# TensorE work laid out product by product behind each burst of scores, with the layer norm and the next stage's start moved

## The chip, the cores and the metric

The kernel runs on one core of one Trainium2 chip. The metric is device time in microseconds (us), smaller is better. Engines are called as the profile calls them: PE is TensorE (matmuls), PEld its weight loads, DVE is VectorE, ACT is ScalarE, POOL is GpSimd, SP is the engine whose queue issues the DMAs.

## What is computed

The input `x` is 4 batches of 1024 tokens of 512 channels, float32. Four layers follow one another, each with a residual; each has 16 heads of 32 channels and a causal mask:

```
x = x + attn_a(layernorm(x))   # squared scores in place of softmax, divided by their sum, then @ Wo
x = x + ffn(layernorm(x))      # softmax attention; keys and values of a token are those of ONE head,
                               # picked by the argmax of softmax(x @ W_gate.T), values times that gate
x = x + attn_b(layernorm(x))   # softmax attention, one key and one value head shared by all heads,
                               # biases, then an output product
x = x + ffn(layernorm(x))
```

In `attn_a`, queries and keys are normalised per head (`(q*gamma+beta)` less its mean, over its deviation); the kernel folds the mean into the weights and the key's deviation into a scale.

## The kernel before

**Two programs.** One layer of one batch is a *stage*. The first program holds the 4 stages of `attn_a` (kind "squared"), the second the 12 stages of the other three layers (kinds "gated", "mqa", "gated"; the profile's names end in `_squared` and `_soft`). A stage has 4 *phases*, one for each group of 4 heads (NG = 4): 16 phases in the first program, 48 in the second. Phase `ph` belongs to stage `ph // 4`.

**A phase.** It has 10 bursts of scores for keys (`KEY_BURSTS`, event "keys", line 1078, in the second program preceded by line 1075, which lays the row's maximum into PSUM). Each burst fills two pairs of PSUM banks; ACT takes a pair with one exponential (line 775) or with squares (line 781). In the second program 9 bursts of the *next* phase's scores by rows lie between them (`ROW_BURSTS`, event "rows", line 1093); DVE takes their maxima (lines 862 and 867). Three pairs of PSUM banks go round: `need_pairs` makes PE wait at the start of a burst until the first pair of the burst before has been taken. POOL masks the probabilities (line 665) and adds them up (lines 678 to 688).

**Other TensorE work.** Everything else goes through two work banks of PSUM, one *unit* after the other, in turn: `av` (probabilities times values, line 1131, in the parts A, B and C), `sm` (sums, line 1106), `mxt` (transposed maxima, line 1197), `rs` and `rw` (line 1204, 1211), `ln` (transposes of the normalised tile, line 1139), `q`, `q2`, `k2` (queries and keys, line 1039), `kvar` (key variance, line 1182, after `ksq`, squares by POOL, line 721), `v2` (line 1174), `gt`, `gtt`, `kall`, `vall`, `kt` (gate logits, all keys and all values of a token block, keys transposed: lines 1052, 1162, 1046, 1190), `ks`, `vs`, `vst` (shared keys and values), `out` (line 1227 or 1229). A unit opens when the unit before the last has been taken out of its bank by ACT or DVE (`free`). In the list of the first program there are 272 units, in that of the second 952. Events without a unit: `load`, `rload` (DMAs), `stats` (DVE statistics at lines 884 to 887, POOL normalises the tile in place at lines 654 and 656), `add`, `mxr`, `gate`, `gate_exp`, `gate_value`.

**The order.** `plan` writes one list of events; every engine walks it in order and does its own part of each event. A phase is 20 *halves*: half 2k opens with the burst of keys k, half 2k + 1 with the burst of rows k. `phase` puts at fixed halves what belongs to the phase itself (av, sm, mxt, add and so on). What is free to move, here called filler, stands in `work` as (events, first half, last half), and `spread` deals it out over the 80 halves of a stage: it works out a pace from the weights of `WEIGHT`, the bursts' own weight among them, and issues filler while the half has room. Units named in `HALVED` are cut in two (an event "more" carries the first half of the products). `norm_events` puts the statistics of tile t + 3 just ahead of the transposes of tile t, and the transposes close together. The next stage's loads and layer norm stand in `work` after this stage's filler and the last stage's outputs; its keys and values may not begin before half 2 * HALVES + 5, which is in the stage's third phase:

```
work.append(([("load", s + 1, t) for t in range(TILES)] + norm_events(s + 1), 0, NG * HALVES))
work.append((first + rest, 2 * HALVES + 5, NG * HALVES))
```

`two_banks` sees to it that no more than two units are open: a third that starts ends the oldest one, with all its products, at once; so does any start after another unit has ended inside an open one.

Of the kernel before, what the change touches and what calls it, by code (L numbers as in the profile page):

```python
# [11 lines left out]
P = 128  # L12
# [66 lines left out]
HALVED = ("av", "q", "q2", "k2", "v2", "ks", "kall", "vall")  # L79
# [24 lines left out]
def features(ph):  # L104
    return [(u, ph, c) for c in range(NC) for u in ("q2", "k2", "ksq")] + [("kvar", ph, c) for c in range(NC)]


def keys_and_values(kind, s):

    if kind == "squared":  # L110
        first = [("v2", s, pair, n) for pair in range(2) for n in range(NT // 2)] + features(4 * s)
        return first, features(4 * s + 1)
# [7 lines left out]
    first = [("ks", s, 0), ("ks", s, 1)] + queries[0] + [("vs", s, 0), ("vs", s, 1), ("vst", s, 0), ("vst", s, 1)]  # L120
    return first, queries[1]


def halved(event, kinds):
    return event[0] in HALVED or event[0] == "out" and kinds[event[1]] != "gated"


def in_halves(events, kinds):
    return [e for event in events for e in ([("more", event)] if halved(event, kinds) else []) + [event]]


def weight(event, kinds):
    if event[0] == "more":
        return weight(event[1], kinds)
    share = 0.5 if halved(event, kinds) else 1.0
    if event[0] == "out":
        return share * (0.9 if kinds[event[1]] == "gated" else 3.5)
    return share * WEIGHT.get(event[0], 0.0)
# [11 lines left out]
def phase(kinds, ph):  # L150

    s = ph // NG
    at = [[] for _ in range(HALVES)]
    more = ph + 1 < NG * len(kinds) and kinds[(ph + 1) // NG] != "squared"
    for k in range(NKB):
        at[2 * k].append(("keys", ph, k))
        if more and k < NRB:
            at[2 * k + 1].append(("rows", ph + 1, k))
    if kinds[s] != "squared":
# [1132 lines left out]
```

How the kernel before makes its waits and increments, by code:

```python
        @block.gpsimd  # L355
# [1 line left out]
            pool.memset(k["ident"][:], 0.0).then_inc(sg.built, 1)  # L357
            pool.memset(k["ident16"][:], 0.0).then_inc(sg.built, 1)
            pool.memset(k["mask"][:], 0.0).then_inc(sg.built, 1)
            pool.memset(k["head_mean"][:], 1.0 / D).then_inc(sg.built, 1)
            pool.memset(k["ones"][:], 1.0)
            pool.memset(k["ones16"][:], 1.0)
            pool.memset(k["minus_half"][:], -0.5)
            pool.memset(k["eps2"][:], EPS * EPS)
            pool.iota(k["rank"][:], pattern=[[0, NT], [-1, HEADS]], base=HEADS, channel_multiplier=0,
                      allow_small_or_imprecise_dtypes=True)
            pool.wait_ge(sg.built, 4)
            for name in ("ident", "ident16"):
                pool.affine_select(out=k[name][:], in_=k[name][:], compare_op=ALU.not_equal, fill=1.0, base=0,
                                   pattern=[[-1, P]], channel_multiplier=1).then_inc(sg.built, 1)
# [2 lines left out]
            pool.affine_select(out=k["head_mean"][:], in_=k["head_mean"][:], compare_op=ALU.is_ge, fill=0.0, base=0,  # L373
                               pattern=[[-D, HG], [0, D]], channel_multiplier=1).then_inc(sg.built, 1)
            pool.wait_ge(sg.built, 7)
            pool.affine_select(out=k["head_mean"][:], in_=k["head_mean"][:], compare_op=ALU.is_ge, fill=0.0,
# [49 lines left out]
        @block.tensor  # L426
        def _(pe):
            pe.wait_ge(sg.loaded, everything)
            pe.wait_ge(sg.vector_step, 1)
            for u in range(2 * KC):
```

## Time and profile before

| | |
|---|---|
| median of 3 runs | 4739.77 us (4738.4 to 4744.24) |
| the profiled execution's own time | 4741.89 us |
| its span, first to last instruction | 4740.1 us |
| busy share of the span: PE, DVE, ACT, POOL | 81%, 40%, 34%, 63% |
| mean granted TensorE clock | 0.918 of full |

Busy time is the union of an engine's instructions. For a wait the profile names the instruction that ended it. A granted clock of 0.918 is a mean over two levels, full and half; a stretch with 0.90 has spent a fifth of itself at half.

### The profile page before, as it was taken

How to read it: one execution, taken by the hardware profiler on the slowest of the kernel's cores; microseconds unless marked ns; L12 is line 12 of the kernel's file. 1: busy time of each engine (PE TensorE's matmuls, PEld its weight loads, DVE VectorE, ACT ScalarE, POOL GpSimd, SP SyncE). 2: the span in 40 equal slices, each digit the busy share in tenths (PEclk: the TensorE clock that was granted, in tenths of full speed). 3: DMA queues.
4: the chain of work that ended last, by engine and by line, in shares of the span. 5: the costliest groups of instructions: out<-in, count | busy, mean ns of one | idle time of the engine just before them, and what ended most of it. 6: DMA issues, size and time to landing. Idle time of an engine off the chain costs nothing. (4 is left out here: it accounts for less than half of the span.)

```text
span 4740.1 us, 66857 instructions
## 1 busy us (share of the span) xinstructions
PE 3849.7 (81%) x26018; PEld 1585.2 (33%) x26018; DVE 1899.4 (40%) x4874; ACT 1630.1 (34%) x2433; POOL 2991.2 (63%) x2215
## 2 busy tenths in 40 slices
PE   6788888985978688688786888888798886977975
PEld 4343434322333233233232333333333332323332
DVE  1212212222544444444444445444544444544452
ACT  1543444551223223323333333333233233232333
POOL 2967777983254646547676676776557466465587
PEclk9899998987989889899898999999899997988998
DMA  1001010003000100100101010010001001010010
GB/s 62 18 1 37 18 36 19 19 19 103 18 1 1 54 1 8 48 1 21 34 17 38 1 34 21 23 32 25 30 1 54 1 19 36 1 53 2 1 37 27
DMA packets 63382, 115.05 MB, mean 24 GB/s; under 512 B 8672, under 2 KB 9184, under 8 KB 63072
## 3 DMA queue, kind: packets, MB, share of 16 engines
q1 hardware_dynamic: 63072, 110.77, 7.2%
q8 instruction: 212, 3.47, 0.3%
q14 instruction: 98, 0.80, 0.1%
HBM read 77.19 MB, written 33.55 MB: 23 GB/s over the span
## 5 line engine op out<-in xcount | busy, mean ns | idle before, releaser
L775 ACT ACTIVATE probs_soft<-banks 128x1024 f32<-128x1024 f32 (+1 forms) x960 | 848.6, 936 | 1426.0 <-PE banks L1078 1411.1
L688 POOL TENSOR_TENSOR added_soft<-added_soft,probs_soft 128x2048 f32<-128x2048 f32 (+3 forms) x384 | 1163.9, 3031 | 67.0 <-ACT probs_soft L775 47.9
L867 DVE CUSTOM_DVE_ANT_0 banks<-banks,mask 128x128 f32<-128x128 f32 (+3 forms) x1536 | 700.7, 525 | 739.1 <-PE banks L1093 739.1
L862 DVE TENSOR_REDUCE maxima_soft<-banks 128x2 f32<-128x1024 f32 x384 | 452.4, 1221 | 527.1 <-PE banks L1093 527.1
L1093 PE MATMUL banks<-k_soft,q_soft 32*128 32x512 f32 (+3 forms) x4608 | 531.4, 555 | 140.4 <-ACT probs_soft L775 140.3
L781 ACT ACTIVATE probs_squared<-banks,key_scale_squared 128x512 f32<-128x512 f32 (+3 forms) x768 | 379.2, 590 | 382.5 <-PE banks L1078 371.6
L665 POOL TENSOR_SCALAR_AFFINE_SELECT probs_soft<-probs_soft 128x512 f32<-128x512 f32 x384 | 239.7, 637 | 427.7 <-ACT probs_soft L775 427.6
L1078 PE MATMUL banks<-q_soft,k_soft 32*128 32x512 f32 (+3 forms) x4608 | 505.7, 521 | 0.0
L1131 PE MATMUL banks<-probs_soft,v_soft 128*32 128x512 f32 (+3 forms) x4608 | 454.2, 514 | 46.0 <-POOL probs_soft L665 31.7
L688 POOL TENSOR_TENSOR added_squared<-added_squared,probs_squared 128x2048 f32<-128x2048 f32 (+3 forms) x128 | 390.2, 3048 | 7.3 <-ACT probs_squared L781 1.9
L1075 PE MATMUL banks<-shift_soft,ones 32*128 32x512 bf16 (+3 forms) x2304 | 205.4, 344 | 227.2 <-DVE maxima_soft L867 136.4
L1093 PEld LDWEIGHTS banks<-k_soft,q_soft 32*128 32x128 f32 x4608 | 198.0, 199 | 378.6 <-issue 372.3
L681 POOL TENSOR_TENSOR added_soft<-probs_soft 128x2048 f32<-128x2048 f32 x48 | 216.8, 4518 | 123.0 <-ACT probs_soft L775 123.0
L1039 PE MATMUL banks<-xnT_soft,g_wq 128*128 128x512 f32 x512 | 254.9, 629 | 33.4 <-DVE scaled_out_soft L990 30.1
L1046 PE MATMUL banks<-g_wv,xnT_soft 128*128 128x512 f32 x512 | 247.9, 615 | 7.1 <-ACT k_soft L758 2.9
L1139 PE MATMUL banks<-ident,tiles_soft 128*128 128x128 f32 x384 | 81.2, 360 | 202.3 <-POOL tiles_soft L656 202.3
L1131 PEld LDWEIGHTS banks<-probs_soft,v_soft 128*32 128x32 f32 x4608 | 125.1, 112 | 353.7 <-issue 260.2
L1075 PEld LDWEIGHTS banks<-shift_soft,ones 32*128 32x128 bf16 x2304 | 64.9, 92 | 524.4 <-issue 505.0
L697 POOL CAST shift_cols_soft<-minus_max_soft 128x16 bf16<-128x16 f32 x96 | 24.4, 255 | 333.4 <-DVE minus_max_soft L875 333.4
L1078 PEld LDWEIGHTS banks<-q_soft,k_soft 32*128 32x128 f32 x4608 | 223.1, 195 | 25.6 <-issue 21.0
L1046 PE MATMUL banks<-g_wk,xnT_soft 128*128 128x512 f32 x512 | 223.8, 595 | 9.6 <-DVE picking_soft L846 9.6
L867 DVE DVE_READ_ACCUMULATOR2_ANT maxima_soft<- 128x1 f32 x1536 | 215.5, 140 | 0.0
(153 smaller groups left out, 4801.0 us busy)
## 6 DMA issues: line engine op xcount, KB each, us to landing
tiles_soft<-out SPq DMA_DIRECT2D x96, 256.0 KB, 2.9
rest_soft<-out SPq DMA_DIRECT2D x96, 256.0 KB, 3.0
out<-rest_soft SPq DMA_DIRECT2D x96, 256.0 KB, 2.1
tiles_squared<-in_x SPq DMA_DIRECT2D x32, 256.0 KB, 2.9
rest_squared<-in_x SPq DMA_DIRECT2D x32, 256.0 KB, 3.2
out<-rest_squared SPq DMA_DIRECT2D x32, 256.0 KB, 2.0
raw_wq<-in_squared_wq SPq DMA_DIRECT2D x1, 1024.0 KB, 5.6
raw_wk<-in_squared_wk SPq DMA_DIRECT2D x1, 1024.0 KB, 7.9
```

What stands on the lines that cost most here:

```text
L665: ins = pool.affine_select(out=cells, in_=cells, compare_op=ALU.is_ge, fill=0.0, base=0, pattern=[[0, HG], [1, P]], channel_multiplier=-1)
L688: ins = pool.tensor_tensor(sums, sums, slot(ph, n)[:, :, col:col + width], ALU.add)
L775: ins = act.activation(slot(ph, n)[:, 2 * a:2 * a + 2, 0:width], score_pair(e, a)[:, :, 0:width], ACT.Exp, scale=SCALE)
L781: ins = act.activation(slot(ph, n)[:, i, col:col + cols], score_pair(e, a)[:, x, col:col + cols], ACT.Square, scale=m["key_scale"][:, ph % ...
L862: ins = dve.reduce_max(m["maxima"][:, ph % 2, 2 * a:2 * a + 2, t, p], score_pair(e, a)[:, :, col:col + width], AX_X)
L867: ins = dve.tensor_tensor_reduce(scores, scores, k["mask"][:, CHUNK - width:CHUNK], 1.0, MASKED, ALU.add, ALU.max, m["maxima"][:, ph % 2, ...
L1039: ins = pe.matmul(out, wt[:, kc, cols], m["xnT"][:, kc, CHUNK * c:CHUNK * c + CHUNK], start=(kc == 0), stop=(kc == KC - 1))
L1046: ins = pe.matmul(out, m["xnT"][:, kc, P * t:P * t + P], wt[:, kc, cols], start=(kc == 0), stop=(kc == KC - 1))
L1075: pe.matmul(psum[:, score_bank(e, i), col:col + width], k["ones16"][D * i:D * i + D, :], m["shift"][D * i:D * i + D, ph % 2, c, q0:q0 + wi ...
L1078: ins = pe.matmul(psum[:, score_bank(e, i), col:col + width], k_of(ph)[D * i:D * i + D, P * kb:P * kb + P], m["q"][D * i:D * i + D, ph % N ...
L1093: ins = pe.matmul(psum[:, score_bank(e, i), col:col + P * blocks], m["q"][D * i:D * i + D, ph % NG, P * t:P * t + P], k_of(ph)[D * i:D * i ...
L1131: ins = pe.matmul(out[D * i:D * i + D, q0:q0 + width], left, slot(ph, n)[:, i, col:col + width], start=(x == 0), stop=(x == len(products) ...
```

## The change

The filler is cut into single products in place of halves (`PIECES`; `share` issues one product for each "more" and the rest at the end). `spread` no longer gives each half the same share: the share is now in proportion to a room per half, taken from `KEYS_TAKEN` and `ROWS_TAKEN` by the size of the burst, and the bursts' own weight is no longer counted. The fixed halves of `av` are kept, as two "more" in the first half and the rest in the second. The first half at which an event may stand comes from a new function `since`, per event: next-stage queries of group 0 from the second phase, those of group 1 from the third, everything that writes nothing in use from the start; the next stage is no longer held back to half 2 * HALVES + 5. The loads and the first four statistics of the next stage get places of their own at the stage's start; the transposes of tiles 0 to 3 alternate with the last stage's outputs 4 to 7, those of tiles 4 to 7 with parts of the next stage's first units. In the squared kind, `k2` and `ksq` now go before `q2`. In the gated kind, units of queries stand between the gate's steps, and `vall` comes last. ACT's guard at the first `ln` of a stage names `q2` in place of `k2`, as that is now the last reader.

```
-HALVED = ("av", "q", "q2", "k2", "v2", "ks", "kall", "vall")
+PIECES = {"av": 4, "q": KC, "q2": KC, "k2": KC, "v2": 2, "ks": KC, "kall": KC, "vall": KC}
+KEYS_TAKEN = {512: 1.25, 256: 0.85}
+ROWS_TAKEN = {P * n: (masked, plain) for n, masked, plain in ((1, 0.95, 0.4), (2, 1.2, 0.65), (3, 1.45, 0.95), (4, 1.75, 1.25))}

-def norm_events(s):
-    events = [("stats", s, t) for t in range(3)]
+def norm_events(s, between):
+    head = [("load", s, t) for t in range(TILES)], [("stats", s, t) for t in range(TILES)]
+    steps = []
     for t in range(NT):
-        if t + 3 < NT:
-            events.append(("stats", s, t + 3))
-        events.append(("ln", s, t))
-        if t + TILES < NT:
-            events.append(("load", s, t + TILES))
-    return events
+        steps.append([("ln", s, t)] + [("load", s, t + TILES)] * (t + TILES < NT))
+        if t >= 2 and t + 2 < NT:
+            steps[-1].append(("stats", s, t + 2))
+    between = [between[n::NT] for n in range(NT)] if len(between) > NT else [between[n:n + 1] for n in range(NT)]
+    return head, [steps[t] + between[t] for t in range(NT)]

 def features(ph):
-    return [(u, ph, c) for c in range(NC) for u in ("q2", "k2", "ksq")] + [("kvar", ph, c) for c in range(NC)]
+    return [(u, ph, c) for us in (("k2", "ksq"), ("q2",)) for c in range(NC) for u in us] + [("kvar", ph, c) for c in range(NC)]
...
-        first = [("gt", s, 0), ("gt", s, 1), ("gtt", s, 0), ("gtt", s, 1), ("gate", s), ("gate_exp", s), ("gate_value", s)]
+        first = [("gt", s, 1), ("gtt", s, 0), queries[0][0], ("gtt", s, 1), ("gate", s), ("gate_exp", s), queries[0][1], ("gate_value", s)]
         first += [("kall", s, t) for t in range(NT)]
         first.insert(len(first) - 2, ("krep", s, 0))
-        first += [("krep", s, 1), ("kt", s, 0)] + queries[0] + [("kt", s, 1)]
-        return first, [("vall", s, t) for t in range(NT)] + queries[1]
+        first += [("krep", s, 1), queries[1][0], ("kt", s, 0), queries[1][1], ("kt", s, 1)]
+        return [("gt", s, 0)], first, [("vall", s, t) for t in range(NT)]
...
+def since(event):
+    event = event[1] if event[0] == "more" else event
+    if event[0] in ("q", "q2", "k2"):
+        return (event[1] % NG + 1) * HALVES if event[1] % NG < 2 else 0
+    if event[0] == "v2":
+        return 2 * HALVES + 3 if event[2] else 3
+    return 0
...
-            pace = max(pace, (ahead + sum(fixed[n:until])) / (until - n))
-        room = carry + pace - fixed[n]
+            pace = max(pace, (ahead + sum(fixed[n:until])) / sum(rooms[n:until]))
+        room = carry + pace * rooms[n] - fixed[n]
...
+            behind = outs[half:]
+            merged = []
+            for t in range(NT // 2):
+                of = next((n for n, e in enumerate(behind) if e[0] == "out"), len(behind) - 1) + 1
+                merged += steps[t] + behind[:of]
+                behind = behind[of:]
+            merged += behind
+            later = []
+            for t in range(NT // 2):
+                later += between[t:t + 1] + steps[NT // 2 + t]
...
+            own = [[("q", 4 * s + g, c) for c in range(NC)] for g in (2, 3)]
+            work = [(head[0], 1), (own[0], HALVES - 2), (outs[:half], 2 * HALVES - 2), (head[1], 2 * HALVES - 2),
+                    (own[1], 2 * HALVES - 2), (merged, 2 * HALVES + 6)]
+        work.append((later + first + rest, NG * HALVES))
+        events += spread(kinds, halves, rooms, work)
...
-                terms = list(enumerate(terms))
+                terms, done = list(enumerate(terms)), begun.get(e, 0)
                 if opening:
-                    begun.add(e)
-                    return terms[:len(terms) // 2]
-                return terms[len(terms) // 2:] if e in begun else terms
+                    begun[e] = done + 1
+                    return terms[done:done + 1]
+                return terms[done:]
```

## Rows read from the trace of the kernel before

**Rows 1.** The page's busy times, then span and mean granted clock.

```profile
PE 3849.7 (81%) x26018; PEld 1585.2 (33%) x26018; DVE 1899.4 (40%) x4874; ACT 1630.1 (34%) x2433; POOL 2991.2 (63%) x2215
...
core 0: 4740.1 us, clock 0.918
```

**Rows 2.** Who waited for whom, PE alone: us in total, times, longest.

```profile
PE banks L1139 <- POOL tiles_soft L656: 202.3, 47, 30.8
PE banks L1093 <- ACT probs_soft L775: 140.3, 186, 1.3
PE banks L1075 <- DVE maxima_soft L867: 136.4, 128, 3.7
PE banks L1075 <- DVE maxima_soft L862: 74.5, 64, 1.9
PE banks L1182 <- POOL key_square_squared L721: 52.2, 14, 7.7
...
PE banks L1039 <- DVE scaled_out_soft L990: 32.6, 5, 7.9
...
PE banks L1139 <- POOL tiles_squared L656: 29.1, 14, 7.0
...
PE banks L1075 <- ACT probs_soft L775: 15.8, 22, 1.3
```

**Rows 3.** Phases 5-7, second program: length, busy PE, PEld, DVE, ACT, POOL, clock, DMA.

```profile
1639.30:1696.00 56.70, 41.58 (x373) 14.75 (x373) 25.75 (x77) 21.16 (x27) 32.96 (x24) 0.83 0.00 1
1696.00:1802.50 106.50, 97.50 (x520) 39.01 (x520) 49.22 (x112) 24.94 (x34) 44.89 (x36) 0.93 0.00 1
1802.50:1861.40 58.90, 52.54 (x409) 19.51 (x408) 31.02 (x85) 21.54 (x27) 36.67 (x29) 1.00 0.00 1
```

**Rows 4.** PE in order of time, phase 5: start, us, instructions [idle before <-releaser].

```profile
1657.59 1.94 PE L1078 MATMUL banks<-q_soft,k_soft 32*128 32x512 f32 x8
...
1663.35 0.40 PE L1075 MATMUL banks<-shift_soft,ones 32*128 32x512 bf16 x4 [1.40 <-DVE maxima_soft L862]
1663.56 1.04 PE L1078 MATMUL banks<-q_soft,k_soft 32*128 32x512 f32 x8
```

**Rows 5.** The same view, phase 3, where filler lies between the bursts.

```profile
1498.62 1.98 PE L1039 MATMUL banks<-xnT_soft,g_wq 128*128 128x512 f32 x4
1500.54 1.15 PE L1093 MATMUL banks<-k_soft,q_soft 32*128 32x256 f32 x16
...
1513.16 1.71 PE L1131 MATMUL banks<-probs_soft,v_soft 128*32 128x512 f32 x16 [0.50 <-ACT shift_soft L758]
```

**Rows 6.** The same view, phase 2: products without a burst between them.

```profile
1392.74 7.03 PE L1046 MATMUL banks<-g_wk,xnT_soft 128*128 128x512 f32 x16
```

**Rows 7.** All engines in order of time, around the first layer norm tile of stage 4.

```profile
2254.56 7.01 SPq L619 DMA_DIRECT2D tiles_soft<-out  x5
...
2260.13 1.08 PE L1139 MATMUL banks<-ident,tiles_soft 128*128 128x128 f32 x4 [18.97 <-POOL tiles_soft L656]
```

**Rows 8.** The same view in the first program: key squares behind a sum.

```profile
344.97 4.50 POOL L688 TENSOR_TENSOR added_squared<-added_squared,probs_squared 128x2048 f32<-128x2048 f32 x1
...
350.61 1.84 PE L1182 MATMUL banks<-head_mean,key_square_squared 128*128 128x4 f32 x8 [6.50 <-POOL key_square_squared L721]
```

**Rows 9.** DVE in order of time: first and last step of a gate.

```profile
1393.47 0.28 DVE L900 TENSOR_REDUCE logit_max_soft<-raw_logits_soft 128x8 f32<-128x128 f32 x1
...
1400.85 0.69 DVE L846 TENSOR_TENSOR picking_soft<-banks,chosen_soft 128x512 f32<-128x512 f32 x1
```

**Rows 10.** Waits of PE in the prologues, 0 to 116 us and 1070 to 1260 us.

```profile
PE banks L1139 <- POOL tiles_squared L656: 10.3, 8, 7.0
...
PE banks L1139 <- POOL tiles_soft L656: 34.3, 8, 30.8
```

**Rows 11.** Busy time by stretch (columns of rows 3): first stage, and the last.

```profile
115.50:352.40 236.90, 197.89 (x1163) 92.41 (x1162) 52.27 (x65) 118.34 (x231) 193.20 (x114) 0.91 0.03 10
...
4493.80:4695.40 201.60, 154.30 (x1437) 59.51 (x1436) 83.30 (x242) 84.78 (x106) 161.98 (x113) 0.94 0.07 22
```

More of the change, by code:

```diff
@@ L119, in keys_and_values @@
-        return first, [("vall", s, t) for t in range(NT)] + queries[1]
[L120 to L129, printed above, removed]
+        first += [("krep", s, 1), queries[1][0], ("kt", s, 0), queries[1][1], ("kt", s, 1)]
@@ new lines, in keys_and_values, with pieces, in_pieces @@
+        return [("gt", s, 0)], first, [("vall", s, t) for t in range(NT)]
+    first = [("ks", s, 1), ("vs", s, 1), ("vst", s, 0), queries[0][1], ("vst", s, 1)] + queries[1]
+    return [("ks", s, 0), ("vs", s, 0), queries[0][0]], first, []
+def pieces(event, kinds):
+    if event[0] == "out" and kinds[event[1]] != "gated":
+        return NG
+    return PIECES.get(event[0], 1)
+def in_pieces(events, kinds):
+    return [e for event in events for e in [("more", event)] * (pieces(event, kinds) - 1) + [event]]
@@ L134, in weight, with taken @@
         return weight(event[1], kinds)
-    share = 0.5 if halved(event, kinds) else 1.0
     if event[0] == "out":
-        return share * (0.9 if kinds[event[1]] == "gated" else 3.5)
-    return share * WEIGHT.get(event[0], 0.0)
+        return (0.9 if kinds[event[1]] == "gated" else 3.5) / pieces(event, kinds)
+    return WEIGHT.get(event[0], 0.0) / pieces(event, kinds)
+def taken(n):
+    return sum(ROWS_TAKEN[P * blocks][0 if p == t // TPC else 1] for t, p, blocks, col in ROW_BURSTS[n]) + 0.15
 def sums_done(kind, ph, c):
@@ L153, in phase @@
     at = [[] for _ in range(HALVES)]
+    room = [KEYS_TAKEN[sum(p[2] for p in KEY_BURSTS[h // 2][2])] for h in range(HALVES)]
     more = ph + 1 < NG * len(kinds) and kinds[(ph + 1) // NG] != "squared"
@@ L177, in phase @@
         h = VALUES_AT[part]
-        at[h].append(("more", ("av", of, part)))
-        at[h + 1].append(("av", of, part))
+        at[h] += [("more", ("av", of, part))] * 2
+        at[h + 1] += [("more", ("av", of, part)), ("av", of, part)]
     for c in range(NC):
@@ L186, in phase, with spread @@
             at[SUMS_AT[c] + later].append(event)
-    return at
-def spread(kinds, halves, work):
-    fixed = [sum(weight(e, kinds) for e in h) for h in halves]
-    queue = [(e, since, until) for part, since, until in work for e in in_halves(part, kinds)]
+    return at, room
+def since(event):
[5 more added lines that the diff above has]
+    return 0
+def spread(kinds, halves, rooms, work):
+    fixed = [sum(weight(e, kinds) for e in h if e[0] not in ("keys", "rows")) for h in halves]
+    queue = [(e, since(e), until) for part, until in work for e in in_pieces(part, kinds)]
     events, carry = [], 0.0
@@ L205, in spread @@
             events.append(queue.pop(0)[0])
-        carry = max(room, 0.0) if queue else 0.0
+        carry = max(room, 0.0) if queue and queue[0][1] <= n else 0.0
     return events + [e for e, _, _ in queue]
@@ L221, in two_banks @@
     for e in events:
-        starts = e[0] == "more" or e[0] in UNITS and e not in since and e not in ended
+        if e[0] == "more" and e[1] in ended:
+            continue
+        starts = e[0] == "more" and e[1] not in since or e[0] in UNITS and e not in since and e not in ended
         while starts and since and (len(since) == 2 or since[next(iter(since))]):
@@ L238, in plan @@
     soft = kinds[0] != "squared"
-    first, rest = keys_and_values(kinds[0], 0)
-    events = [("load", 0, t) for t in range(TILES)] + norm_events(0) + first
+    between, first, rest = keys_and_values(kinds[0], 0)
+    head, steps = norm_events(0, [])
+    events = head[0] + head[1] + [e for step in steps for e in step] + between + first
     if soft:
@@ L252, in plan @@
     for s in range(stages):
-        halves = [h for g in range(NG) for h in phase(kinds, NG * s + g)]
+        phases = [phase(kinds, NG * s + g) for g in range(NG)]
+        halves = [h for at, _ in phases for h in at]
+        rooms = [x for _, room in phases for x in room]
         outs = [("out", s - 1, t) for t in range(NT)] if s else []
```

31 lines of the change are left out of this document (16 added, 15 removed).

## The prediction, made before the changed kernel had run

> **What bounds the kernel now.** I read the busy times first: PE is busy for 3849.7 us of a span of 4740.1, POOL for 2991.2, and the granted clock is 0.918 [rows 1]. So PE sets the time, in three parts: its work at full clock, some 890 us of idle time, and what half clock adds. Then I read who ended PE's idle time [rows 2]. It falls into four kinds. **Burst waits**: a burst of scores waits until ACT or DVE has taken the first pair of the burst before: 140.3 + 136.4 + 74.5 + 15.8 = 367 us in the second program. **Layer norm**: the transposes wait for POOL's normalised tile, 202.3 + 29.1 = 231 us. **Key variance**: 52.2 us. **Outputs**: 32.6 us. Then I read the stretches [rows 3] to see where filler lies. Phase 5 has none: 56.7 us with 41.6 busy, 15.1 idle, clock 0.83. Phase 6 has a dump of it (106.5 us, 97.5 busy), phase 7 an even share (58.9 us, 52.5 busy, clock 1.00). Phase 7 does 11 us more work than phase 5 in 2.2 us more time: filler between bursts is almost free there. Last, the order of time shows the wait that it replaces: 1.40 us before a burst without filler [rows 4], none before the bursts around a half unit of queries [rows 5].
>
> **The terms.** Each is against the profiled execution (4741.9 us, its span 4740.1 and 1.8 around it).
>
> Burst waits. Phases 5 to 7 hold 97.5 + 52.5 - 2 × 41.6 = 67 us of filler [rows 3], 1.1 us for each of their 60 gaps, near the 1.40 of a wait [rows 4]. Two products of a query unit are one insertion of 1.92 us [rows 5], so one product is near 0.9 and leaves at most half a microsecond of the wait; rooms in proportion give the masked bursts more. Nothing changes where no next stage follows, in the last stage of the second program, which sits idle for 201.6 - 154.3 = 47 us [rows 11]: 40 us of it are burst waits by my estimate and stay. In the other 44 phases I keep 1.6 us each, since an av, sum or transpose that starts ends an open unit at once (two banks), and its gap-mates stay bare: 70 us. Of 367 go **257**. The ends: 327 if every gap is filled, 100 if units mostly collapse.
>
> Layer norm. One tile waited 19 us [rows 7]: the loads of the next tiles stood in SP's queue behind the stores of the last outputs, whose sums stood on POOL behind sums of probabilities; they went at 2254.6, then came statistics, POOL, and PE at 2260.1. The change issues these loads at the stage's start, the statistics ahead of own queries, and puts an output between two transposes. The two prologues keep their 10.3 + 34.3 [rows 10], as nothing lies beside them. Of the rest I keep 30 us, for tiles 4 to 7, whose POOL steps still queue behind sums of 4.5 us [rows 8]. Of 231 go **157**. Ends: 187 and 90.
> Moved with them, on SP: loads of tiles 4 to 7 now alternate with the output stores and wait for those in turn; each has a fill of a few microseconds before its statistics, which covers it; if that cover is gone, DVE waits on the tile with row maxima behind it, and this is the 90.
>
> Key variance. `kvar` of both chunks stands right behind the last `ksq`, which sits behind a 4.50 us sum; PE waits 6.50 [rows 8]. With two query units between them, some 8 products of 0.9 us and their bursts, the squares are done first. Of 52 go **40**; ends 52 and 20.
>
> Outputs. The first four of a gated stage still come close together, each through DVE and then POOL behind its sums. I keep all 32.6 [rows 2], as the weight of an output is as before. Ends: 20 less, 20 more.
>
> Clock. The mean of 0.918 is 0.082 × 2 × 4740 = 777 us at half clock. The same eight matmuls take 1.94 us there and 1.04 at full [rows 4], so each busy microsecond at half loses half of itself: between 0 and 389 us. PE is busy for 81% of the span, but the falls follow its waits; I take 60%, 233 us lost. Idle time goes down by 257 + 157 + 40 of 890, about half; stretch by stretch, less idle means a higher clock (0.83, 0.93, 1.00 in rows 3). I let the loss fall to 126: **107** go. Ends: 60 and 180.
>
> What it adds. **Gate**: DVE takes 7.4 us from the first to the last step [rows 9]. Today a run of key products covers most of it, PE has 7.03 us of them in one piece [rows 6]; afterwards only a query unit and bursts lie there, and row maxima queue behind the gate on DVE. 3.5 us in each of 7 stages that are followed by a gated one: **+25** (0 to 45). **Alternation**: 16 matmuls in one run take 7.03 us, 0.44 each [rows 6]; four between two bursts take 1.92 from their start to the burst's [rows 5], so a run inserted costs about 0.16 to 0.2. Of 1070 gaps 547 have no filler today; some 350 will: **+70**. Ends: 0, as part of it falls into today's waits, and 110.
> Here a rule of the Trainium skill speaks against the change. "TensorEngine Tiling (Array Packing)", Key Properties, says that going from one tiling mode to another drains TensorE; bursts (32 rows) and products (128) are two modes, and more, smaller runs mean more drains. It gives no price; "TensorE: Matmul & The Clock Gate", in its section on a single matmul, has some 175 ns for a drain, and as my estimate two drains a run would make the term 120 in place of 70 and the time about 4325.
>
> Costed at nothing: the cut of `av` (same two gaps as before), `vall` last (needed only in the next stage), `q2` in ACT's guard. POOL stays under the bound: in phases 5 to 7 it has 115 us against 192 of PE [rows 3]. It is near the bound in the first stage alone, 193 us against 198 [rows 11], which therefore cannot fall far below 205.
>
> **Sum**: 257 + 157 + 40 + 107 - 25 - 70 = 466 us. 4741.9 - 466 = 4276; the median of the runs lies 2.1 lower, so 4274.
>
> **Rivals.** *It stays lumpy* (the change does not do what it says). With the two-bank rule, and 9 or more fixed units in each 20 halves, most cut units are closed early. Then the burst waits lose 100 alone, the clock 45, alternation costs 25: 4740 - 100 - 157 - 40 - 45 + 25 + 25 = 4448. For it: an open unit of four pieces spans about three halves, in which one or two others start. Against it: phase 7 is even already, with whole halves.
> *Every gap fills.* Waits go by 327, the norm by 187, the clock by 180, alternation and gate cost 40: 4740 - 327 - 187 - 52 - 180 + 40 = 4034. For it: phase 7's clock of 1.00. Against it: POOL's share of the first program.
> *Slower: the work banks bind.* A unit that stays open over three gaps leaves one bank to all others, and each opening then waits for ACT or DVE to take out the last one, 0.50 us where it happens today [rows 5]. There are 1224 units. At 0.50 each that is 612 us and the time 4274 + 612 = 4886; it decides for slower above 466 / 1224 = 0.38 us a unit. Against it: half units stand open over a burst today, and such waits are a small part of PE's list.
>
> **Numbers.** Forecast 0.50, its own range 4170 to 4380 by the ends of the terms that go together; lumpy 0.22; every gap 0.20; banks 0.05; 0.03 for a mixture near no change. The range of 8 in 10 reaches over most of the two neighbours: 4090 to 4470. A difference under 0.2% (9 us) can't be told from none in a measurement of this kernel. Faster by more 0.94, within 0.01, slower 0.05.
>
> **What would show it.** PE busy about as now less the clock's loss, with idle near 450 us; layer norm waits under 90 us, most of it in the prologues; burst waits near 110 and key variance near 12; granted clock near 0.95; phases 4 to 7 of the second program within 10 us of one another, near 65; a DVE wait of row maxima behind the gate, once a stage. It is wrong if the burst waits stay above 200 (lumpy), if waits of lines 1039, 1046 and 1131 for ACT or DVE grow past 200 us (banks), or if the norm's waits only move to another line.

## The result, and the profile after

| | before | after |
|---|---|---|
| median of the runs | 4739.57 us (4738.4 to 4744.24) | 4504.73 us (4503.83 to 4507.83) |
| ratio | | 0.9504, 95% interval 0.9487 to 0.952 |
| span of the profiled execution | 4740.1 us | 4502.5 us |
| mean granted TensorE clock | 0.918 | 0.941 |

Faster by 235 us: half of the forecast gain of 466, and outside the range by 35 us. Of one later kernel, `p1_apart_stats`, two of the four executions ran at a lower clock than the others and are left out; no other time here has such an execution in it. In the kernel after, lines stand 42 further down than before: the bursts of keys are 1117 and 1120, those of rows 1135, `q` 1081, `kall` 1088, `av` 1173, `ln` 1181, a gated `out` 1269, `sm` 1148.

Busy times, and below them span and clock, of the kernel after (answers to [rows 1]):

```profile
PE 3828.6 (85%) x26018; PEld 1528.5 (34%) x26018; DVE 1892.7 (42%) x4874; ACT 1628.4 (36%) x2433; POOL 2992.7 (66%) x2215
...
core 0: 4502.5 us, clock 0.941
```

PE still sets the time. Who it waited for, after (us in total, times, longest; answers to [rows 2]):

```profile
PE banks L1135 <- ACT probs_soft L817: 102.3, 139, 1.3
PE banks L1181 <- POOL tiles_soft L698: 87.4, 23, 30.3
PE banks L1117 <- DVE maxima_soft L909: 48.3, 59, 1.9
PE banks L1088 <- DVE picking_soft L888: 47.3, 31, 3.0
PE banks L1117 <- DVE maxima_soft L904: 42.1, 48, 3.3
...
PE banks L1269 <- DVE scaled_out_soft L1032: 36.8, 14, 4.1
PE banks L1181 <- POOL tiles_squared L698: 35.8, 13, 9.6
...
PE banks L1148 <- DVE scaled_out_soft L1032: 19.1, 4, 5.2
...
PE banks L1081 <- DVE raw_logits_soft L934: 9.1, 6, 2.1
PE banks L1117 <- ACT probs_soft L817: 8.5, 12, 1.3
```

The four lines of burst waits come to 201 us, from 367. Layer norm is 123, from 231. The key variance's line is gone. New is what stands between them: `kall` waiting for `picking_soft`, the copy by which DVE takes the `kall` before the last out of its bank. It was 12.2 us before.

For more than the longest lists I sorted every idle time of PE over 0.1 us by who waited and who ended it. The clock loss is half of PE's busy time at half clock; PE work is busy time less that loss. Both are estimates: the eight matmuls of [rows 4] lose 0.90 of 1.94 us at half clock, 46% and not 50%, so the loss may be some 8% too high. In us:

| | before | after | predicted change | measured |
|---|---|---|---|---|
| waits of bursts (both programs) | 385 | 215 | -257 | -170 |
| waits of `ln` for POOL | 231 | 123 | -157 | -108 |
| `kvar` for POOL | 52 | 0 | -40 | -52 |
| units waiting for ACT or DVE to empty a bank ("bank waits") | 89 | 175 | 0 (+25 for the gate) | +86 |
| outputs and what waits behind them ("out chain") | 46 | 71 | 0 | +25 |
| clock loss | 246 | 177 | -107 | -69 |
| PE work at full clock | 3604 | 3652 | +70 | +48 |
| **sum**, with the small rest | | | -466 | -238 |

The stretches that answer to [rows 3], phases 5 to 7 of the second program after (us, then busy and count of PE, PEld, DVE, ACT, POOL, clock, DMA share, GB/s):

```profile
1529.48:1606.10 76.62, 65.20 (x447) 24.27 (x447) 34.48 (x98) 25.21 (x34) 42.61 (x37) 0.89 0.13 39
1606.10:1674.54 68.44, 61.90 (x436) 23.30 (x436) 33.80 (x89) 23.22 (x30) 41.60 (x32) 1.00 0.01 1
1674.54:1741.09 66.55, 59.90 (x423) 21.50 (x423) 33.59 (x89) 20.94 (x26) 37.65 (x29) 1.00 0.00 1
```

The dump of phase 6 is gone, as forecast. With the queries, keys and norm spread out, all three hold about the same work. But the two even phases still have 6.5 and 6.7 us of idle time. In the order of time their waits of over 0.4 us are five of bursts (4.0 us) and seven of units for a bank (8.7 us). An example, PE in phase 5, after:

```profile
1574.08 1.98 PE L1088 MATMUL banks<-g_wk,xnT_soft 128*128 128x512 f32 x4
1576.00 1.14 PE L1135 MATMUL banks<-k_soft,q_soft 32*128 32x512 f32 x8
1577.07 1.13 PE L1088 MATMUL banks<-g_wk,xnT_soft 128*128 128x512 f32 x2
1580.18 1.13 PE L1088 MATMUL banks<-g_wk,xnT_soft 128*128 128x512 f32 x2 [1.99 <-DVE picking_soft L888]
1581.24 0.52 PE L1117 MATMUL banks<-shift_soft,ones 32*128 32x512 bf16 x4
```

The product that starts at 1577.07 is the last of one `kall`. The next product opens another `kall`, in the same gap, and waits 1.99 us. Its bank is the one in which that last product had just ended, although nothing stands in the other. The kernel gives the two banks in turn, in the order in which units *end*, and the sums (line 1148, run at 1583.39) begin after this `kall` but end before it: the empty bank is kept for them. In the list of the kernel after, 246 units open in the gap in which their own bank's last unit ended (240 before). In 90 of these cases (39 before) the unit of the other bank has not begun; in 11 (2 before) it is open; in the rest it has ended. DVE in the same stretch shows what the wait is made of:

```profile
1577.17 2.36 DVE L904 TENSOR_REDUCE maxima_soft<-banks 128x2 f32<-128x1024 f32 x2 [3.42 <-PE banks L1135]
1579.45 0.68 DVE L888 TENSOR_TENSOR picking_soft<-banks,chosen_soft 128x512 f32<-128x512 f32 x1
```

The copy itself takes 0.68 us. Before it DVE takes the maxima of the row burst that has just ended, until 1579.5: an opening right behind its bank's last unit waits for both. Over both programs, outputs left aside, units wait 98 us for a bank that DVE empties, and during 39 us of them DVE is at row maxima; before the change it was 2 of 46 us.

### The profile page after: what moved, and what is told of

It reads as the page before. It is cut to its first block, busy times and chain, and to the rows that moved or that the text cites. A ratio compares the mean times of both kernels' runs of the same rounds, so it can differ in the third digit from the quotient of the medians.

```text
span 4502.5 us, 67228 instructions
## 1 busy us (share of the span) xinstructions
PE 3828.6 (85%) x26018; PEld 1528.5 (34%) x26018; DVE 1892.7 (42%) x4874; ACT 1628.4 (36%) x2433; POOL 2992.7 (66%) x2215
## 4 chain that ended last, share of the span: by engine, by line
PE 52%; DVE 8%; POOL 6%; ACT 5%; issue 4%; DMA 0%; POOLq 0%; DVEq 0%; ACTq 0%
PE banks L1135 10%; PE banks L1088 10%; PE banks L1120 8%; PE banks L1173 8%; PE banks L1081 7%; ACT probs_soft L817 4%; DVE banks L909 4%; POOL added_soft L730 3%; PE banks L1117 3%; DVE maxima_soft L904 2%; PE banks L1271 2%; PE banks L1148 1%; DVE maxima_soft L909 1%; PE banks L1246 1%; POOL tiles_soft L698 1%
## 5 line engine op out<-in xcount | busy, mean ns | idle before, releaser
L1135 PE MATMUL banks<-k_soft,q_soft 32*128 32x512 f32 (+3 forms) x4608 | 509.5, 534 | 102.4 <-ACT probs_soft L817 102.3
L1135 PEld LDWEIGHTS banks<-k_soft,q_soft 32*128 32x128 f32 x4608 | 185.6, 189 | 337.6 <-issue 331.4
L1088 PE MATMUL banks<-g_wv,xnT_soft 128*128 128x512 f32 x512 | 259.3, 625 | 40.8 <-DVE picking_soft L888 34.5
L1081 PE MATMUL banks<-xnT_soft,g_wq 128*128 128x512 f32 x512 | 266.7, 639 | 22.1 <-DVE raw_logits_soft L934 9.1
L1088 PE MATMUL banks<-g_wk,xnT_soft 128*128 128x512 f32 x512 | 250.6, 615 | 22.9 <-DVE picking_soft L888 12.8
L1120 PE MATMUL banks<-q_squared,k_squared 32*128 32x512 f32 (+3 forms) x1536 | 177.8, 549 | 13.6 <-ACT probs_squared L823 13.6
```

The costliest lines, as they stand in the source:

```text
L1081: ins = pe.matmul(out, wt[:, kc, cols], m["xnT"][:, kc, CHUNK * c:CHUNK * c + CHUNK], start=(kc == 0), stop=(kc == KC - 1))
L1088: ins = pe.matmul(out, m["xnT"][:, kc, P * t:P * t + P], wt[:, kc, cols], start=(kc == 0), stop=(kc == KC - 1))
L1120: ins = pe.matmul(psum[:, score_bank(e, i), col:col + width], k_of(ph)[D * i:D * i + D, P * kb:P * kb + P], m["q"][D * i:D * i + D, ph % N ...
L1135: ins = pe.matmul(psum[:, score_bank(e, i), col:col + P * blocks], m["q"][D * i:D * i + D, ph % NG, P * t:P * t + P], k_of(ph)[D * i:D * i ...
```

## The experiments

There are fifteen kernels, measured in four groups, each beside the kernel before, whose median was 4743.3, 4741.2, 4742.0 and 4741.7 us. **A gap** is the time between two bursts (1070 of them), bare if no filler lies in it; av, sums, maxima and what follows the sums have fixed places and are no filler. Columns are us of one profiled execution, sorted as above; `p1_apart_stats` is told in the text alone. "Cut" is into how many parts a unit goes.

| kernel | cut | median us | ratio (95%) | bursts | norm | bank | out chain | clock loss | PE work |
|---|---|---|---|---|---|---|---|---|---|
| before | halves | 4739.6 | 1 | 385 | 231 | 89 | 46 | 246 | 3604 |
| after | single, rooms | 4504.7 | .9504 (.9487-.952) | 215 | 123 | 175 | 71 | 177 | 3652 |
| layout_only | single, rooms | 4815.5 | 1.0159 (1.0129-1.0188) | 314 | 247 | 161 | 46 | 263 | 3635 |
| order_only | halves | 4383.5 | .9244 (.9225-.9262) | 274 | 138 | 96 | 50 | 133 | 3622 |
| pieces2 | halves, rooms | 4396.6 | .9273 (.9251-.9295) | 250 | 124 | 93 | 69 | 138 | 3626 |
| flat | single | 4512.9 | .9517 (.95-.9534) | 262 | 119 | 198 | 57 | 168 | 3646 |
| pieces1 | whole | 4358.3 | .9194 (.9172-.9217) | 381 | 128 | 44 | 16 | 122 | 3588 |
| p1_rooms | whole, rooms | 4461.1 | .9404 (.939-.9418) | 360 | 148 | 30 | 42 | 161 | 3589 |
| order_hold | halves | 4684.4 | .9881 (.9857-.9906) | 378 | 176 | 120 | 63 | 246 | 3614 |
| old_norm | halves | 4505.1 | .95 (.9477-.9523) | 279 | 240 | 93 | 47 | 147 | 3623 |
| outs_apart | single, rooms | 4453.9 | .9388 (.9367-.9409) | 232 | 107 | 177 | 29 | 138 | 3653 |
| p1_stats | whole | 4365.3 | .9202 (.9187-.9217) | 388 | 121 | 43 | 18 | 134 | 3588 |
| late_open | single, rooms | 4348.3 | .9164 (.9151-.9178) | 227 | 117 | 56 | 64 | 148 | 3635 |
| late_apart | single, rooms | 4315.9 | .9101 (.9088-.9115) | 243 | 105 | 59 | 27 | 128 | 3637 |
| o_late | halves | 4297.2 | .9061 (.9047-.9074) | 295 | 138 | 45 | 18 | 112 | 3613 |
| o_apart_late | halves | 4260.1 | .8981 (.8966-.8996) | 253 | 131 | 38 | 35 | 111 | 3613 |

**Order against layout.** The change is two things, and I took them apart. `order_only` is the changed kernel with the old layout:

```
-PIECES = {"av": 4, "q": KC, "q2": KC, "k2": KC, "v2": 2, "ks": KC, "kall": KC, "vall": KC}
+PIECES = {"av": 2, "q": 2, "q2": 2, "k2": 2, "v2": 2, "ks": 2, "kall": 2, "vall": 2}
...
-    room = [KEYS_TAKEN[sum(p[2] for p in KEY_BURSTS[h // 2][2])] for h in range(HALVES)]
+    room = [1.0] * HALVES
...
-    fixed = [sum(weight(e, kinds) for e in h if e[0] not in ("keys", "rows")) for h in halves]
+    fixed = [sum(weight(e, kinds) for e in h) for h in halves]
...
-                    return terms[done:done + 1]
+                    return terms[:len(terms) // 2]
```

> The changed kernel's order (early start, norm between outputs, keys before queries) with the old layout: half units, the same share for every half, burst weights counted. Gaps between bursts that hold no filler: 547 before, 321 after the change, 409 here. Theory A (burst waits follow the bare gaps, 0.70 us before and 0.67 after for each): burst waits 280 us, norm waits near the changed kernel's 123, and with 137 fewer runs of other work between bursts than the changed kernel some 25 us less PE work; time 4530, so the order brings most of the gain. Theory B (the single products bring it): burst waits stay above 330 and the time above 4600.

Measured 4383.5, 147 us under theory A's time, though its burst waits (274) and PE work came out as it said: the order alone takes 356 us, and the layout on top of it gives 121 back. `layout_only` is the reverse, the kernel before with single products and rooms, the next stage's first part due by the end of the third phase and outputs 4 to 7 from half 14:

> The kernel before with the change's layout alone (single products, rooms by burst), its old order kept but for one thing that keeps it free of a deadlock: the next stage's first part must be done by the end of the third phase, outputs 4 to 7 start at half 14 or later. Gaps without filler 436 against 547. Theory A (after four runs: the order gives the gain, the fine cut trades burst waits for bank waits, more runs and clock): burst waits 290 to 310 in place of 385, bank waits up from 89 to 170, norm and key variance waits stay at 231 and 52, PE work 35 us up; time 4765, so not faster than before. Theory B (the fine cut is good by itself and only clashes with the new order): 4650 or less.

Measured 4815.5, slower than before by 1.6% and 50 us over theory A. So the part that gives the change its name costs time on top of the new order, and gains none with the old one; how much of the 1.6% belongs to the deadline that this kernel adds was not separated. The waits of PE in `layout_only`:

```profile
PE banks L1109 <- ACT probs_soft L791: 112.9, 156, 1.3
PE banks L1091 <- DVE maxima_soft L883: 94.8, 89, 2.2
PE banks L1091 <- DVE maxima_soft L878: 69.9, 60, 1.9
...
PE banks L1062 <- DVE picking_soft L862: 44.2, 31, 4.7
```

It does take burst waits away (385 to 314), and pays 72 us of bank waits and 31 of PE work for them.

**Cut and rooms one at a time.** `pieces2` is the changed kernel with halves (of the diff above, the lines of `PIECES` and `terms`); `flat` keeps single products and drops the rooms (the lines of `room` and `fixed`).

> The changed kernel with units cut in halves in place of single products, rooms by burst size kept. 396 gaps without filler against 321. Theory A: burst waits 268 us in place of 215, idle for a bank of the work pair less than 175 (156 openings right after their bank's last unit ended, against 246), PE work some 25 us less (126 fewer runs); in sum 4500, within 20 of the changed kernel: cutting finer gives with one hand what it takes with the other. Theory B (fine cuts are what counts): 4560 or more.

> The changed kernel with single products but the same share for every half and the bursts' weight counted, as before. 334 gaps without filler against 321. Theory A: burst waits 225, time 4515. Theory B (shares in proportion to the burst are what hides the masked bursts): burst waits over 260 and the time over 4550.

4396.6 and 4512.9. For `pieces2` both theories were over 100 us too high; for `flat` the time is theory A's, the burst waits (262) are not. It is the cut that costs: halves to single products is +129 without rooms, +108 with them. Rooms alone are +13 and -8, where the 95% intervals overlap: they take 24 and 47 us off the burst waits, which is given back mainly in the out chain (50 to 69, 57 to 71) and where `av` waits for POOL's masks (49 to 70, 41 to 69). `pieces1` goes the other way, units whole:

```
-PIECES = {"av": 2, "q": 2, "q2": 2, "k2": 2, "v2": 2, "ks": 2, "kall": 2, "vall": 2}
+PIECES = {"av": 2}
...
```

> The kernel order_only with whole units in place of halves (av still in two). Gaps without filler 596 against 409, runs of other work between bursts 1243 against 1488. Theory A (a trade with an optimum near halves): burst waits 400 us in place of 274, bank waits near 50 in place of 96, PE work 45 us less; time 4415. If coarser is simply better, 4350 or less; if the burst waits decide alone, 4510.

4358.3: whole units beat halves by 25 us, though their burst waits (381) are as long as before the change. Bare gaps in the lists fall with the cut (596 whole, 409 halves, 334 single), and the burst waits with them, 0.64 to 0.78 us for each bare gap. Against that stand bank waits of 44, 96 and 198, PE work of 3588, 3622 and 3646, and the clock.

`p1_rooms` puts the rooms back over whole units:

> The kernel pieces1 with shares in proportion to the burst. In single products the shares took 47 us off the burst waits, in halves 24, and the time moved by 8 and 13 us (down, up). With whole units, four times the size of a product, the place can hardly follow the room: burst waits within 20 of 381, time 4358 within 15. If the shares matter for the clock or the norm, more than 30 either way.

4461.1, 103 us slower than `pieces1`, where I had said within 15. The profile has the loss in the norm (+20), in outputs (+26), in `av` waiting for POOL's masks (62 to 100, as in the two pairs above) and in the clock (+39); burst waits fell by 21. A pace in small steps cannot be followed with whole units, but why POOL comes late there I did not settle.

**Inside the order.** `order_hold` holds the next stage's keys and values back to half 2 * HALVES + 5 again, and makes their first part due by the end of that third phase, a deadline that neither the kernel before nor `order_only` has; `old_norm` puts the loads, statistics and transposes back behind the outputs, in one piece as in `norm_events` of before; both on `order_only`.

```
     if event[0] in ("q", "q2", "k2"):
-        return (event[1] % NG + 1) * HALVES if event[1] % NG < 2 else 0
-    if event[0] == "v2":
-        return 2 * HALVES + 3 if event[2] else 3
+        return 2 * HALVES + 5 if event[1] % NG < 2 else 0
+    if event[0] in ("v2", "gt", "gtt", "ks", "vs", "kall", "vall"):
+        return 2 * HALVES + 5
...
-        work.append((later + first + rest, NG * HALVES))
+        work += [(later, NG * HALVES), (first, 3 * HALVES), (rest, NG * HALVES)]
```

> The kernel order_only with the next stage's keys and values held back to half 2 * HALVES + 5 again (and its first part due by the end of the third phase); the norm stays as changed. Gaps without filler 491 against 409: by 0.67 us for each, burst waits 329 in place of 274; with the clock some 75 us more, 4460. If the early start is worth nothing by itself, 4385; if it is the main part of the order's gain, 4550 or more.

> The kernel order_only with the old arrangement of the norm: loads, statistics and transposes of the next stage close together behind all outputs; the early start stays. Norm waits go back from 138 to about 231, low clock time up with them: 4500. If the norm's waits only change places, they stay under 160 or other waits fall by as much, and the time is 4400.

4684.4 and 4505.1: the first is 224 us over my forecast, in the branch "the main part of the order's gain", the second is as forecast. The early start is worth 301 us against a start held back with that deadline (burst waits 378 to 274, clock loss 246 to 133, norm 176 to 138), the norm's place 122. The lists show what the early start does: by the weights, the four phases of the second program's first three stages hold 26, 0, 62 and 15 us of filler before the change, 26, 0, 49 and 28 in `order_hold`, and 29, 28, 26 and 20 in `order_only`. A start held back without the deadline was not run, so how much of the 301 us is the deadline's stays open. With 356 for both and the reordered `k2`, they overlap. PE's longest waits in `old_norm`, then in `order_only`:

```profile
PE banks L1184 <- POOL tiles_soft L701: 198.9, 49, 30.6
PE banks L1138 <- ACT probs_soft L820: 108.7, 151, 1.3
```

```profile
PE banks L1134 <- ACT probs_soft L816: 111.4, 159, 1.3
PE banks L1180 <- POOL tiles_soft L697: 101.8, 24, 30.4
```

Of these the norm's line is the one that differs: 49 waits against 24.

**Outputs.** After the change the wait that [rows 2] has at line 1039 is at 1269 and 1148. PE in phase 4, after:

```profile
1466.44 1.10 PE L1269 MATMUL banks<-ident,y_soft 128*128 128x128 f32 x8
1470.57 1.25 PE L1269 MATMUL banks<-ident,y_soft 128*128 128x128 f32 x8 [3.03 <-DVE scaled_out_soft L1032]
1471.76 0.39 PE L1117 MATMUL banks<-shift_soft,ones 32*128 32x512 bf16 x4
1471.98 1.74 PE L1120 MATMUL banks<-q_soft,k_soft 32*128 32x512 f32 x8
1478.95 1.94 PE L1148 MATMUL banks<-added_soft,ones 128*32 128x512 f32 x8 [5.22 <-DVE scaled_out_soft L1032]
```

Four outputs (two records of two) lie in one gap: the third waits 3.03 us for the copy of the first, which DVE begins at 1469.83, after the row maxima of the burst before; the sums behind them wait 5.22. `outs_apart` changes one weight, so that one output fills a gap:

```
-        return (0.9 if kinds[event[1]] == "gated" else 3.5) / pieces(event, kinds)
+        return (2.4 if kinds[event[1]] == "gated" else 3.5) / pieces(event, kinds)
```

> The changed kernel with the weight of a gated output raised from 0.9 to 2.4, so that four of them no longer go into one gap. If the output chain (PE, DVE, POOL behind sums, two buffers) stalls PE because outputs come faster than POOL serves them, its 71 us of waits fall below 30, low clock time falls with them, and the time is 4450. If POOL is late whatever the spacing, the waits stay near 70 and only move, and the time stays 4505 within 10.

4453.9, 51 us less than after; the out chain 71 to 29, the clock loss 177 to 138. It is as theory A said.

**The bank.** `late_open` tests the reading of the wait at 1580 us. It is the changed kernel with one more pass over the list: the first product of a unit in parts is moved behind the next burst where the unit two before it, which had the same bank, ended in the same gap; further products of that unit in that gap go with it. In the lists 156 openings move, with 73 further products, each by one gap. Nothing else moves, and no product is dropped.

```
+        if e[0] == "more" and of not in opened:
+            opened.add(of)
+            if by_number.get(unit[of] - 2) in recent:
+                held.append(e)
+                continue
...
```

> The changed kernel; a unit whose bank's last unit has ended in the same gap opens one gap later. Such openings fall from 246 to 90. Theory A (a unit that stays open over several gaps makes its successor share its bank, and the successor opens before ACT or DVE has taken it out): bank waits fall from 175 us to 80, with less half clock; time 4410. Theory B (ACT and DVE are late whatever PE does, the wait only moves to the burst behind it): bank waits fall, burst waits rise from 215 to 300, time 4500.

4348.3, 156 us less than after and 62 under theory A. With the pass, 90 of the 246 openings stay, nearly all of them of units in one piece, which the pass leaves where they are. All cases in which the other bank stood empty are gone. PE in the same part of the stage, in `late_open`:

```profile
1559.41 1.98 PE L1120 MATMUL banks<-g_wk,xnT_soft 128*128 128x512 f32 x4
1561.33 1.14 PE L1167 MATMUL banks<-k_soft,q_soft 32*128 32x512 f32 x8
1562.40 2.84 PE L1120 MATMUL banks<-g_wk,xnT_soft 128*128 128x512 f32 x6
1565.17 0.29 PE L1149 MATMUL banks<-shift_soft,ones 32*128 32x256 bf16 x4
```

The gaps hold two and three products, with no wait; and over the whole program:

```profile
PE banks L1167 <- ACT probs_soft L849: 98.5, 134, 1.3
...
PE banks L1120 <- DVE picking_soft L920: 5.8, 14, 1.0
```

`kall` waits 5.8 us for `picking_soft` where it waited 47.3. All bank waits fall by 119 us (175 to 56), PE's sorted idle time by 117 in all: what went did not come back as another wait. Of the waits that DVE still ends, 35 us counted as above, it is at row maxima for 2 us in place of 39. The rest is clock loss (177 to 148) and PE work (3652 to 3635).

**Loads and statistics.** Tiles 4 to 7 still wait. All engines in phase 5, after:

```profile
1533.05 7.87 SPq L661 DMA_DIRECT2D tiles_soft<-out  x3
...
1533.19 4.76 POOL L730 TENSOR_TENSOR added_soft<-added_soft,probs_soft 128x1536 f32<-128x1536 f32 x2
1533.23 0.69 DVE L926 BATCH_NORM_STATS2 stats_soft<-tiles_soft 128x6 f32<-128x512 f32 x1 [7.61 <-DMA tiles_soft<-out]
...
1538.56 0.77 POOL L698 TENSOR_SCALAR tiles_soft<-tiles_soft,minus_mean_soft,rstd_soft 128x512 f32<-128x512 f32 x1
...
1539.47 1.08 PE L1181 MATMUL banks<-ident,tiles_soft 128*128 128x128 f32 x4 [6.84 <-POOL tiles_soft L698]
```

DVE begins the statistics at 1533.2, as the load lands; POOL has just begun two sums, 4.76 us together, and normalises at 1538.6. `p1_stats` moves the statistics of a tile one transpose earlier (`t + 3` for `t + 2`), to tell a late DVE from a queued POOL:

> The kernel pieces1 with the statistics of tiles 4 to 7 one step earlier (tile t + 3 behind the transposes of tile t). Theory A (the norm waits that are left, 128 us less 45 in the prologues, are statistics that start too late): norm waits 90, time 4325. Theory B (they are POOL's queue of sums, or DVE now waits for the load with row maxima behind it): norm waits stay at 125 or burst waits rise, time 4350 to 4380.

4365.3 against 4358.3, within the intervals, the norm 128 to 121: nothing, as theory B said. Earlier statistics did not help here; that POOL's queue of sums is what remains fits the rows above, but no run took it away. `p1_apart_stats` added an output weight of 1.8 to that:

> The kernel p1_stats with the weight of a gated output raised from 0.9 to 1.8. In pieces1 the output chain waits 16 us in place of 71 in the changed kernel, so little is left to gain there: time within 15 of p1_stats. If spacing the outputs also spaces the transposes between them (they alternate), the norm waits fall by 20 more and the time is 4300.

It took 4390 and 4391 us (ratio 0.9257, 0.9238 to 0.9275), 25 us more than `p1_stats`, where I had said within 15. With whole units the out chain is 16 to 18 us already, so spreading outputs out has little left to take; why it cost 25 us was not settled.

**Together.** If the price of a cut is the opening, halves pay it too:

> Halves (old layout, new order) with the openings moved. Theory A (the price of a cut is the opening behind the bank's own last unit, and halves pay a smaller part of it, 96 us of bank waits against 44 with whole units): bank waits fall to about 50, time 4383 - 60 = 4320, ratio 0.911, so that single products (4348) keep no lead over halves. Theory B (with the openings moved the finer cut is the better one, as the change means it): halves gain 15 or less and end at 4368 or more, over the 4348 of single products.

> The changed kernel with both repairs: an opening moved behind the next burst where its bank's last unit ended in the same gap, and the weight of a gated stage's output 2.4 in place of 0.9. Theory A (two separate costs, openings 157 us and outputs 51 us, that lie in different gaps): about 4300 us, ratio 0.908, out chain near 20 us of waits, bank waits near 55. Theory B (what held the outputs was the same shared bank, so the first repair has taken it already): 4340 to 4355, out chain falls but burst waits or bank waits rise by as much.

> Halves, new order, openings moved, outputs apart (weight 2.4). Theory A (costs add up): o_late less 35 to 50, about 4280, ratio 0.903, the fastest of all. Theory B (they overlap, or outputs spread out delay the next layer norm, which waits on POOL's copies of them): not under 4320.

4297.2, 4315.9 and 4260.1. Moving the openings, 73 of them, is worth 86 us with halves, and they stay ahead of single products with the same repair by 51, and ahead of whole units by 61 (whole units with it were not run; only one of their openings is of a unit in parts). The waits of PE in `o_late` and `late_open` over the bursts show what single products still buy, 161 us of waits for DVE's maxima against 106:

```profile
PE banks L1148 <- DVE maxima_soft L940: 91.4, 95, 1.9
PE banks L1148 <- DVE maxima_soft L935: 69.7, 47, 6.3
```

```profile
PE banks L1149 <- DVE maxima_soft L936: 54.3, 75, 3.3
PE banks L1149 <- DVE maxima_soft L941: 51.8, 58, 1.9
```

Single products have 68 us less of burst waits and 21 less of the norm's, but 46 more in the out chain, 21 more in `av` behind POOL, 11 more bank waits, 22 more of PE work and 36 more of clock loss. `late_apart` fell between its theories (32 us for outputs apart, where 51 were taken without the other repair), `o_apart_late` fell by 37 against `o_late`, as expected. `o_apart_late` is the fastest kernel here: 0.898 of before and 245 us under the change. It has the change's order, the old halves, the moved openings and the output weight.

## Why the prediction was wrong, point by point

**What failed: the bank.** The forecast had no term for it. The rival *slower: the work banks bind* named the wait, with another mechanism (a unit open over several gaps leaves one bank to all others, which holds for 11 of the 246 openings), and was set aside with "half units stand open over a burst today, and such waits are a small part of PE's list". That is true, and says nothing of four parts in place of two. Measured: 89 to 175 us, +86, which is 0.07 us for each of 1224 units, far under the 0.38 that would have turned the sign. The place was right, the size between nothing and the rival's. A count alone would not have given it: the list of before has 240 openings right behind their own bank's last unit, that of after 246. But if all bank waits are laid on them, those of before cost 89 / 240 = 0.37 us each, those of after 175 / 246 = 0.71, as those of `order_only` (0.61, of 158), `pieces1` (0.73, of 60) and `flat` (0.82, of 240). Two things differ. In the lists, no product at all lies between the end and the opening in 39 cases before and in 90 after, those in which the other bank's unit has not begun; products worth 3 us or more by the weights lie there in 76 cases before and in 3 after. And DVE is at row maxima during 39 us of the waits after, 2 us before. Neither explains `pieces1`, which has one such opening and no such wait, so the price of one opening stays open. `late_open` shows what the openings cost with all that hung on them: 156 us, two thirds of the shortfall of 231.

**Burst waits**, -257 forecast, -166 in the second program (201 left for 110); the term that is furthest off in the table. I left 1.6 us a phase, for gaps made bare by the two-bank rule, and said that some 350 of the 547 bare gaps would get filler: 226 did, 321 stay bare. My sign for *it stays lumpy*, burst waits above 200, is just met (201 in the second program, 215 in both). But the two-bank rule hardly acts: of 1161 cut parts, 76 are closed early, so that rival had the wrong cause, though its 4448 is nearer than the 4274. What is bare is bare for want of filler: of the 321 gaps, 47 are in the last stage, and 30 to 39 in each stage whose next is "mqa" against 12 to 20 in the others of that program. The mqa stage has one key and one value head and less to lay out: by the weights, the program's first three stages hold some 25 us of filler a phase, the fourth, whose next is "mqa", 12. The 215 us of burst waits are 0.67 us for each bare gap, near the 0.70 of before. I had read one gated stage and multiplied it by 44 phases.

**Layer norm**, -157 forecast, -108. The two prologues keep 43.5 us, as said. The rest, 80 us, is 2.7 times the 30 that I kept: `old_norm` shows that the new place is worth 122 us of time; POOL's queue is what the rows and `p1_stats` point to for the remainder, and no run took it away. The bound of 90 was nearer.

**Key variance**, -40 forecast, -52: right, the wait is gone. **Outputs**, 0 forecast, +25: 5 us beyond the end of +20. I argued from an unchanged weight; with it, four outputs land in one gap where the bursts' weight no longer slows the pace, and `outs_apart` gets 51 us back by that weight.

**Clock**, -107 forecast, -69. The loss before was 246 (forecast 233) and is 177. It fell short because idle time did: 69 us of loss went with 217 us of idle time in the span (890 to 674), 0.32 for each; I had forecast 107 for 429, 0.25. So the rate was not too high, the idle time that goes was.

**Gate**, +25 forecast: the row that I asked for, a wait at 1081 for the logits, has 9.1 us in six waits. **Alternation**, +70 forecast, +48 measured: 226 gaps got filler in place of the 350 that I took, which is 0.21 us each, by my 0.16 to 0.2; the price was right and the count was not. In the trace TensorE's products change their tile (32*128, 128*128 or 128*32 in the rows) 2076 times before and 2397 times after, 321 more, 0.15 us each. The Trainium skill's rule ("TensorEngine Tiling (Array Packing)", Key Properties: a change of mode drains TensorE) speaks the same way, and the trace agrees with its sign. At the 175 ns that the Trainium skill's "TensorE: Matmul & The Clock Gate", Single matmul latency, has for a drain, one for each change, 321 changes would make 56 us by my estimate, near the 48 measured. The changes are not all of it: `late_open` has 2402 and 17 us less PE work than after. It was not alternation that halved the gain.

So by the table the bursts are 87 us short, the bank 61 (86 less the 25 given for the gate), the norm 49, the clock 38 and the outputs 25, together 260. Alternation came out 22 better and key variance 12; with 2 us more of small waits, that is the 228 missing.

*Open.* Why single products keep 36 us more of clock loss than halves at nearly the same idle time (`late_open` 541 us of sorted idle time, `o_late` 553), how much of the 301 us of the early start is the deadline of `order_hold`, and why rooms over whole units make POOL late, were not settled.

## What to carry to other kernels

Work laid between the bursts is worth what it hides only if the bank it opens is empty by then, and the engine that empties it may have the burst's own work to do first. Before a unit is cut finer, look in the order for units that open right behind the last user of their own buffer; moving those by one burst gave 86 to 156 us here. Where buffers go by the order of ending, a unit in parts can wait for a full one beside an empty one; giving them by the order of opening is the other repair, and was not run. The place from which filler may be taken counted for more here than how finely it is cut: the order took 356 us, and going from halves to single products lost 108 to 129. And a sample of one stage kind is no basis for a sum over three.

## What I had not expected of the hardware

A finer cut made PE's own work dearer even at full clock: the same 26018 matmuls cost 3588 us with whole units, 3622 with halves and 3646 with single products; from whole to halves that is 34 us for 180 more changes of tile (2089 to 2269), 0.19 us each, and on to single products 24 us for 67 more, 0.36 each. As the price is not the same, and `late_open` shows less PE work at as many changes, what the rest is made of stays open. And the clock loss moved by up to 36 us between kernels of nearly equal idle time (above), so idle time in total does not tell it.
